# A state-space layer whose scale and shift are read from PSUM, with the skip weight in the kernel's first tap and the residual added on TensorE

## The chip, the cores and the metric

The kernel runs on one core of one Trainium2 chip. The metric is device time in microseconds (us) of one execution, and lower is better. Five engines run side by side: TensorE (PE in the profile; PEld is its weight load), VectorE (DVE), ScalarE (ACT), GpSimd (POOL) and SyncE (SP), which only issues DMAs here. Each engine executes its own instructions strictly in the order in which they were written; engines meet through semaphores.

## The reference

A two-layer decoder over x of 2 batches x 512 tokens x 128 features: a gated recurrence, cross attention, latent attention with an expert mixture, a selective state-space scan, the layer that is edited here, and a second expert mixture. Each is added to its input and normalised. The edited layer, per batch:

```python
c_t = attn_mean @ V                                    # attention over the context
x = layernorm(x_text, g_norm_in, b_norm_in)
scale_in, shift_in = split(c_t @ W_film_in + b_film_in, 2)
x = x * (1.0 + mod_gate * scale_in) + mod_gate * shift_in
y = irfft(rfft(x, 2*L) * rfft(K, 2*L))[:L] + x * D_skip  # K: 512 taps per feature, from 64 complex states
scale_out, shift_out = split(c_t @ W_film_out + b_film_out, 2)
y = y * (1.0 + mod_gate * scale_out) + mod_gate * shift_out
xt = x_text + y
h = layernorm(xt, g_ffn, b_ffn)
xt = xt + gelu(h @ W1 + b1) @ W2 + b2
return layernorm(xt, g_norm_out, b_norm_out)
```

The caller adds the layer's input once more and normalises (ln5).

## The kernel before

Features lie on the 128 partitions and a batch's 512 tokens along the free axis, so most work is on tiles of 128 x 512 float32: one such tile fills one PSUM bank. The two batches are two **lanes**, a and b, with four PSUM banks each (`own(b, 0)` to `own(b, 3)`) and a set of SBUF tiles (`A(b, n)`; `Xin[b]` is the layer's input). What both need (decay tables, the convolution kernel's taps K and their spectrum) is the shared lane w, which borrows lane a's bank in one place.

Every engine has, for each lane, one program written as a generator: one named **step** (mostly one instruction, or one accumulation group) up to each `yield`. `STEPS` lists the names in order. `done(engine, lane, step)` counts the step on that engine's and lane's semaphore; `after(...)` is the wait for it. An engine's final order is a string in `TURNS`: "a7 w1 a6" takes seven steps of lane a, one of w, six of a (L531 to L535). So a step never runs ahead of an earlier one in its engine's order, ready or not. `TABLES` says before which of ScalarE's steps a table of activation functions (log, gelu, exp, sin; the gates' is sin) is loaded, 42 loads in all (L1204).

Lane a runs ahead of lane b by about one layer. The steps that the change and the prediction touch are these.

- Selective scan, per state i of 16: ScalarE's exponential `aa i`, GpSimd's product `by i` (L2195), VectorE's scan `sc i` (L1878) and product `hc i`; sums of products go on TensorE. `dx` on GpSimd and `rl`, `dl` on VectorE prepare the rows that SP writes to DRAM and reads back spread over the partitions ("AR<-scan"). `X4` and ln4 end it; their result is `Xin`. `s4` adds the residual.
- Kernel taps, lane w: ScalarE's sines and exponentials `eP`, `eQ`; GpSimd's `aP`, `aQ`, `U`, `V` and VectorE's `hu`, `hw`, `P` build two tables for each half; TensorE multiplies them (`kp0`, `kp1`) and ScalarE copies (`kp1`). SP stores the taps in four pieces and loads them back rearranged as `Kdl` (L656 to L663, semaphore `kshuf`), between the rows of lane b's scan. TensorE transposes them (`kt`, L1181 to L1184, in lane a's bank 0) and `kf` makes the spectrum.
- Edited layer, per lane: attention `xb.s` (TensorE, bank 2), `xb.m`, `xb.d`, `xb.u`, `xb.i`, `xb.k`, `xb.p` (VectorE), `xb.t` and the copy `xb.a`; normalised input `lni.x`, `lni.g` in A10; the four products `fl0` to `fl3` (scale in, shift in, scale out, shift out; L1039) into banks 0 to 3; ScalarE's copies `s0` to `s3` with the bias into A4, A5, A6, A8; VectorE's `lni.z` = A10 * A4 and `xin` = A10 + A5 into A2; the transposes `xit`; forward transform `xf0`, `xf1` (L1008); spectrum product `ks`, `kd` (lane a only), `bs` to `yo` (VectorE); inverse transform `inv0`, `inv` (L1061), even and odd tokens in the halves of bank 1; then VectorE's `sk` = A2 * D_skip + bank 1, `fo` = A4 * A6, `fp` = A4 + A8, `xt` = A4 + Xin in two halves. Behind it `lnf` and the feed-forward `w1`, `w2`, `lno`, `s5`, `X5` and ln5.
- Around it: the expert units of the first mixture, with ScalarE's gates `sl` (lane a's end at 236 us), and those of the second (`eg`, gates `el`), which follow the edited layer in each lane.

TensorE's steps of the layer stand at L1022 to L1091, ScalarE's at L1440 to L1482, VectorE's at L1897 to L1996. One line of helpers records most VectorE products (L1553), tensor-scalar operations (L1556), scalar_tensor_tensor (L1559) and reductions (L1562); L1208 is every ScalarE activation and L689 every mean square of a norm. For the edited layer the order of the lanes around 344 us is: lane b's scan ends while lane a is in its transforms, and lane b's layer begins.

Of the kernel before, what the change touches and what calls it, by code (L numbers as in the profile page):

```python
# [22 lines left out]
ALU = mybir.AluOpType  # L23
# [3 lines left out]
B, T, D = 2, 512, 128  # L27
# [37 lines left out]
              "lnf": (3, 0), "lno": (3, 1), "ln5": (3, 2), "ln6": (1, 0), "lnf.c": (2, 1), "ln5.c": (0, 1)}  # L65


def _halves(*names):

    return [n + h for n in names for h, _ in COLS]  # L70
# [93 lines left out]
def _centre(t):  # L164
# [13 lines left out]
        *_halves("ln4.v"), "xb.s", "xb.t", "fl0", "fl1", "fl2", "fl3", "xit",  # L178
# [11 lines left out]
        *_ln("ln4"), "lni.sq", "lni.l", "lni.r", "xb.e", "lni.g", "xb.a", "s0", "s1", "s2", "s3", "xit", "ko", "xo", *_ln("lnf"), *_halves("lnf.g"),  # L190
# [13 lines left out]
        "sk", "fo", "fp", *_halves("xt"), *_halves("lnf.x"), *_halves("lno.x"), *_halves("s5"), *_halves("X5"),  # L204
# [13 lines left out]
            "ed.s", "ed.m"],  # L218
# [15 lines left out]
    "dve":  # L234
# [8 lines left out]
    "act":  # L243
# [6 lines left out]
    "pool":  # L250
        "w12 b3 w1 b2 w1 b1 w37 a1 w1 a4 w1 a7 w1 a4 b1 a1 w1 b16 w1",
# [57 lines left out]
def build(nc, dram, out):  # L309
    lay = layouts()  # L310
    with ExitStack() as ctx:
# [371 lines left out]
        def _(pe):  # L683
# [338 lines left out]
            def state_space(b):  # L1022
# [6 lines left out]
                yield  # L1029
                pe.wait_ge(*after("dve", b, "xb.p"))  # L1030
# [7 lines left out]
                for o in range(4):  # L1038
                    mm(own(b, o), VF[:, b, 128 * o:128 * o + 128], A(b, 3), start=True, stop=True)\  # L1039
                        .then_inc(*done("pe", b, f"fl{o}"))  # L1040
                    yield
                pe.wait_ge(*after("dve", b, "xin"))
                pe.wait_ge(*after("act", b, "s3"))
# [3 lines left out]
                yield  # L1047
                pe.wait_ge(*after("act", b, "xit"))
# [9 lines left out]
                for p in range(2):  # L1058
                    pe.wait_ge(*after("dve", b, ("ye", "yo")[p]))
                    for k in range(NFB):  # L1060
                        last = mm(own(b, 1)[:, HT * p:HT * p + HT], Yf[b][:, NF * p + 128 * k:NF * p + 128 * k + 128],  # L1061
                                  Gh[:, T * k + p:T * k + T:2], start=(k == 0), stop=(k == NFB - 1))
                    last.then_inc(*done("pe", b, ("inv0", "inv")[p]))
                    yield
# [49 lines left out]
            def shared_program():  # L1114
# [66 lines left out]
                pe.wait_ge(kshuf, 16)  # L1181
# [10 lines left out]
        def _(act):  # L1192
# [247 lines left out]
            def state_space(b):  # L1440
# [18 lines left out]
                for o, to in enumerate((4, 5, 6, 8)):  # L1459
                    act.wait_ge(*after("pe", b, f"fl{o}"))  # L1460
                    f(A(b, to), own(b, o), ACT.Identity, (b, f"s{o}"), bias=bfilm[:, o:o + 1])
                    yield
# [88 lines left out]
        def _(dve):  # L1551
# [345 lines left out]
            def state_space(b):  # L1897
# [23 lines left out]
                dve.wait_ge(*after("act", b, "s1"))  # L1921
                tt(A(b, 10), A(b, 10), A(b, 4), ALU.mult, (b, "lni.z"))
                yield
                mine(b, "lni.z")
                tt(A(b, 2), A(b, 10), A(b, 5), ALU.add, (b, "xin"))
# [8 lines left out]
                if not b:  # L1934
# [32 lines left out]
                dve.wait_ge(*after("pe", b, "inv"))  # L1967
                pairs = "p (t two) -> p t two"
                stt(A(b, 4).rearrange(pairs, two=2), A(b, 2).rearrange(pairs, two=2), vec("Ds"),
                    own(b, 1).rearrange("p (two t) -> p t two", two=2), ALU.mult, ALU.add, (b, "sk"))  # L1970
                yield
                mine(b, "sk")
                dve.wait_ge(*after("act", b, "s3"))
                tt(A(b, 4), A(b, 4), A(b, 6), ALU.mult, (b, "fo"))
                yield
                mine(b, "fo")
                tt(A(b, 4), A(b, 4), A(b, 8), ALU.add, (b, "fp"))
                yield
                mine(b, "fp")
                for h, c in COLS:  # L1980
                    tt(A(b, 0)[:, c], A(b, 4)[:, c], Xin[b][:, c], ALU.add, (b, f"xt{h}"))
                    yield
# [59 lines left out]
            def shared_program():  # L2042
# [126 lines left out]
                for h in HALVES:  # L2169
# [15 lines left out]
                    yield  # L2185
                dve.wait_ge(loads["ffn1"], 16)
# [345 lines left out]
```

## Time and profile before

| What | us |
|---|---|
| median of three timed runs | 485.99 (484.13 to 487.59) |
| the profiled execution, its own time | 481.76 |
| its span in the trace | 480.0 |
| TensorE busy | 411.1 (86%) |
| VectorE busy | 331.9 (69%) |
| ScalarE busy | 289.2 (60%) |
| GpSimd busy | 124.9 (26%) |

The span is the time from the first to the last instruction that the profiler records; the execution's own time has 1.8 us more around it. The mean granted clock of TensorE was 0.93 of full speed. Times within the trace are counted from the span's start.

How to read it: a busy share over the whole span says little, because the bound changes from stage to stage. A group row gives the source line, engine, operation, output and inputs by name with partitions x elements, the count, busy time and mean of one; then the idle time of the engine just ahead of such instructions and what ended most of it. A timeline row gives start, duration and, in brackets, the idle time before and its releaser.

### The profile page before, as it was taken

Reading aid. Unit: us, or ns where it says so; the run is one execution under the profiler, and the core shown is the slowest. Engines: PE = TensorE matmul, PEld = TensorE weight load, DVE = VectorE, ACT = ScalarE, POOL = GpSimd, SP = SyncE. Lnnn points to the kernel's source line nnn. Section 1 sums busy time; section 2 is a strip of 40 time slices with the busy share of each in tenths; the row PEclk is TensorE's granted clock in tenths of the full one; section 3 lists DMA queues with packets and bytes.
Section 4 is the critical chain, followed back from the end, with each engine's and each line's share of the span. In section 5 each row is a group of like instructions: output and inputs, shape, how many; then the busy total and the mean of one; then the engine's idle time right before and its main releaser. Section 6 shows DMA issues by size and latency. Waiting matters only on the chain.

```text
span 480.0 us, 5922 instructions
## 1 busy us (share of the span) xinstructions
PE 411.1 (86%) x2035; PEld 201.5 (42%) x2035; DVE 331.9 (69%) x616; ACT 289.2 (60%) x508; POOL 124.9 (26%) x128
## 2 busy tenths in 40 slices
PE   6978988878799999999977884557889899999995
PEld 3444433443345554434443221233666544544442
DVE  1485567799969963562799999899977543574454
ACT  5945697525255678989567897456347576552125
POOL 1200000000482029006965767745100200000000
PEclk9988999988879999999997998657989999999999
DMA  7950000564281000005008967988600001502401
GB/s 262 362 157 32 1 2 0 164 98 152 70 182 17 2 3 4 2 12 165 0 1 231 233 164 222 217 223 253 252 0 1 1 0 22 156 1 54 124 0 44
DMA packets 26109, 46.62 MB, mean 97 GB/s; under 512 B 7397, under 2 KB 12742, under 8 KB 24918
## 3 DMA queue, kind: packets, MB, share of 16 engines
q1 hardware_dynamic: 25972, 46.15, 33.7%
q8 instruction: 16, 0.26, 0.2%
q10 hardware_dynamic: 108, 0.10, 0.1%
q14 instruction: 13, 0.11, 0.1%
HBM read 41.13 MB, written 5.01 MB: 96 GB/s over the span
## 4 chain that ended last, share of the span: by engine, by line
PE 59%; DVE 21%; ACT 10%; issue 6%; POOL 2%; DMA 1%; DVEq 0%; SPq 0%; ACTq 0%
PE PS L925 7%; DVE AR L1553 7%; PE PS L957 6%; ACT AR L1208 6%; PE PS L930 5%; PE PS L853 4%; PE PS L839 4%; ACT L1204 3%; PE PS L689 3%; PE PS L822 3%; DVE stats L1562 3%; DVE AR L1878 3%; PE PS L1008 2%; PE PS L1061 2%; DVE AR L1559 2%
## 5 line engine op out<-in xcount | busy, mean ns | idle before, releaser
L1208 ACT ACTIVATE AR<-PS 128x512 f32<-128x512 f32 (+1 forms) x219 | 110.6, 537 | 109.1 <-PE PS L925 49.3
L1553 DVE TENSOR_TENSOR AR<-PS,AR 128x512 f32<-128x512 f32 (+1 forms) x104 | 69.1, 675 | 49.6 <-PE PS L930 30.6
L2195 POOL TENSOR_TENSOR AR<-AR 128x512 f32<-128x512 f32 (+2 forms) x48 | 52.3, 1097 | 136.0 <-DVE AR L1553 106.4
L1208 ACT ACTIVATE AR<-AR 128x256 f32<-128x256 f32 (+2 forms) x130 | 54.5, 469 | 44.6 <-DVE AR L1553 28.1
L1204 ACT ACT_TABLE_LOAD x42 | 53.9, 1283 | 0.8
L1562 DVE TENSOR_REDUCE stats<-PS 128x1 f32<-128x512 f32 (+4 forms) x88 | 43.6, 521 | 8.7 <-PE PS L763 3.5
L1878 DVE TENSOR_TENSOR_SCAN AR<-PS,AR 128x512 f32<-128x512 f32 x32 | 38.8, 1211 | 0.7 <-POOL AR L2195 0.6
L822 PE MATMUL PS<-RR 97*128 97x512 bf16 (+3 forms) x128 | 33.3, 337 | 5.5 <-DVE stats L1562 3.6
L689 PE MATMUL PS<-AR,W_sq 128*128 128x256 f32 x88 | 27.3, 424 | 10.6 <-ACT AR L1208 6.3
L1553 DVE TENSOR_TENSOR AR<-AR 128x512 f32<-128x512 f32 (+2 forms) x48 | 30.7, 654 | 3.6 <-ACT AR L1208 2.3
L839 PE MATMUL PS<-RR 100*128 100x512 bf16 (+3 forms) x128 | 29.8, 303 | 2.2 <-ACT AR L1208 2.1
L2279 POOL TENSOR_TENSOR RR<-KL,lags 128x512 f32<-128x512 f32 x24 | 29.4, 1263 | 1.2 <-PE PS L842 1.1
L930 PE MATMUL PS<-x_in,RR 128*128 128x512 f32 x56 | 28.6, 596 | 0.0
L957 PE MATMUL PS<-AR,RR 128*128 128x512 f32 x56 | 28.5, 596 | 0.0
L925 PE MATMUL PS<-x_in,RR 128*128 128x512 f32 x56 | 28.4, 595 | 0.0
L1208 ACT ACTIVATE PS<-AR,RA 128x512 f32<-128x512 f32 x32 | 21.5, 685 | 10.3 <-DMA AR<-scan 5.1
L689 PEld LDWEIGHTS PS<-AR,W_sq 128*128 128x128 f32 x88 | 15.9, 201 | 24.8 <-ACT AR L1208 16.2
L825 PE MATMUL PS<-W_bf 128*128 128x256 bf16 (+1 forms) x80 | 22.4, 280 | 0.0
L853 PE MATMUL PS<-AR,Vaug 128*9 128x512 f32 (+3 forms) x256 | 21.8, 434 | 0.0
L842 PE MATMUL PS<-W_bf 128*128 128x256 bf16 (+1 forms) x80 | 20.2, 253 | 0.0
L1710 DVE TENSOR_REDUCE stats<-PS 128x1 f32<-128x384 f32 x32 | 17.5, 548 | 3.5 <-PE PS L825 3.3
L822 PEld LDWEIGHTS PS<-RR 97*128 97x128 bf16 x128 | 11.5, 105 | 20.0 <-DVE stats L1562 11.0
(239 smaller groups left out, 697.5 us busy)
## 6 DMA issues: line engine op xcount, KB each, us to landing
AR<-scan SPq DMA_DIRECT2D x64, 256.0 KB, 4.0
RR<-in_ffn SPq DMA_DIRECT2D x1, 2688.0 KB, 11.5
RR<-in_ones SPq DMA_DIRECT2D x2, 832.0 KB
RR<-in_ones SPq DMA_DIRECT2D x2, 784.0 KB
RA<-in_moe SPq DMA_DIRECT2D x1, 1539.5 KB, 6.4
AR<-weights SPq DMA_DIRECT2D x6, 256.0 KB, 4.7
W_mla<-in_mla SPq DMA_DIRECT2D x1, 1504.0 KB, 15.3
W_late<-in_late SPq DMA_DIRECT2D x1, 1076.0 KB, 11.8
```

The lines of the kernel that those rows point to most:

```text
L689: mm(own(b, i)[:, c], w("sq", "ones"), A(b, 1)[:, c], start=True, stop=True)\
L822: mm(ring[:, c:c + n_], Qst[b][0:MROWS, h, 128 * qt:128 * qt + 128], Kst[b][0:MROWS, h, 0:n_], start=(qt, c) == segs[0][1:], stop=False)
L839: mm(ring[:, c:c + n_], Kst[b][0:KROWS, h, 128 * kb:128 * kb + 128], Qst[b][0:KROWS, h, 128 * kb:T], start=(c == 0), stop=False)
L925: mm(own(b, 0), w(group, "g", 128 * k, 128), x, start=True, stop=True)\
L930: mm(own(b, 1), w(group, "u", 128 * k, 128), x, start=True, stop=True)\
L957: mm(own(b, 3), w(group, "d", 128 * j, 128), A(b, 6 + j % 2), start=(j == 0 and base is None), stop=(k == n))\
L1204: nc.scalar.preload_act_table_set(tables[loaded[0]])
L1208: nc.scalar.activation(out_, in_, func, bias=bias, scale=scale).then_inc(*done("act", *step))
L1553: nc.vector.tensor_tensor(out_, a, b_, op).then_inc(*done("dve", *step))
L1562: nc.vector.tensor_reduce(out_, a, X, op).then_inc(*done("dve", *step))
L1878: nc.vector.tensor_tensor_scan(A(b, 14 + i % 2), own(b, 1 + 2 * (i % 2)), scan_row(b, "dx", i), 0.0, ALU.mult, ALU.add).then_inc(*done("dv ...
L2195: nc.gpsimd.tensor_tensor(out_, a, b_, op).then_inc(*done("pool", *step))
```

## The change

- **Scale and shift in.** `s0` and `s1` go. VectorE's `lni.z` and `xin` become scalar_tensor_tensor, which read the products fl0 and fl1 where TensorE left them (banks 0 and 1) and add the bias themselves.
- **Scale and shift out.** The order of the products becomes fl0, fl1, fl3, fl2; fl3 goes to bank 2 and fl2 to bank 3, and ScalarE copies fl3 first, then fl2.
- **The input.** A new TensorE step `fx` multiplies `Xin` by the identity into bank 2 and leaves the sum open; fl3 is added to it. So A8 holds shift out plus x_text, and `xt` adds A8 in place of `Xin`; `fp` goes.
- **The skip weight.** A new VectorE step `kD` (lane w) adds half of D_skip to the first column of `Kdl`, once the rows are loaded back; the transform's later steps hold a factor of two. TensorE's `kt` waits for `kD`. `sk` goes.
- **Two halves.** The odd tokens of the inverse transform go to bank 3. `fo0` and `fo` multiply the even and the odd tokens, 128 x 256 each, from PSUM by A6 into every second column of A4.
- **New turns.** All four strings of `TURNS` are new from the first step on, and `TABLES` with them: 48 loads for 42. Moves beside the edited steps, as the two strings give them: VectorE takes b's hc3 ahead of a's X4, b's sc5 and hc5 ahead of a's xb.m, the shared P1 ahead of a's sc11 and so of b's rl and dl, hu3, hw3, hu4 and hw4 ahead of a's sc4, a's yi ahead of b's X4, a's ye and yo ahead of b's xb.m, and a's fo0 and fo ahead of b's xb.p. GpSimd takes dx, by0 and by1 of lane a ahead of aP1, by2 to by4 ahead of aQ1, and U11, U21, V1 later between the by's; the chain of decay products (dc1 to dc23) ahead of lane b's split of keys and queries. ScalarE takes kp1 ahead of b's aa2, and part of lane b's norm f1 (its log and root) in between a's gates sl4 to sl7, with a table load ahead of each of the two and one behind it. TensorE takes a's lnf.c ahead of b's fl0.

```diff
+FILM_BANKS, FILM_TURNS = (0, 1, 3, 2), (0, 1, 3, 2)
...
-        *_halves("ln4.v"), "xb.s", "xb.t", "fl0", "fl1", "fl2", "fl3", "xit",
+        *_halves("ln4.v"), "xb.s", "fx", "xb.t", "fl0", "fl1", "fl3", "fl2", "xit",
...
-        "sk", "fo", "fp", *_halves("xt"), ...
+        "fo0", "fo", *_halves("xt"), ...
...                                              (TensorE, state_space)
+                pe.wait_ge(*after("dve", b, "xb.d"))
+                mm(own(b, 2), w("sq", "id"), Xin[b][:, :], start=True, stop=False).then_inc(*done("pe", b, "fx"))
+                yield
...
-                for o in range(4):
-                    mm(own(b, o), VF[:, b, 128 * o:128 * o + 128], A(b, 3), start=True, stop=True)\
+                for o in FILM_TURNS:
+                    mm(own(b, FILM_BANKS[o]), VF[:, b, 128 * o:128 * o + 128], A(b, 3), start=(o != 3), stop=True)\
                         .then_inc(*done("pe", b, f"fl{o}"))
                     yield
+                pe.wait_ge(*after("act", b, "s3"))
                 pe.wait_ge(*after("dve", b, "xin"))
-                pe.wait_ge(*after("act", b, "s3"))
...
+                pe.wait_ge(*after("act", b, "s2"))
                 pe.wait_ge(*after("act", b, "xit"))
...
-                        last = mm(own(b, 1)[:, HT * p:HT * p + HT], Yf[b][...],
+                        last = mm(own(b, (1, 3)[p])[:, HT * p:HT * p + HT], Yf[b][...],
...                                              (TensorE, shared lane)
-                pe.wait_ge(kshuf, 16)
+                pe.wait_ge(*after("dve", "w", "kD"))
                 pe.wait_ge(*after("act", "w", "kp1"))
...                                              (ScalarE)
-                for o, to in enumerate((4, 5, 6, 8)):
+                for o, to in ((3, 8), (2, 6)):
                     act.wait_ge(*after("pe", b, f"fl{o}"))
-                    f(A(b, to), own(b, o), ACT.Identity, (b, f"s{o}"), bias=bfilm[:, o:o + 1])
+                    f(A(b, to), own(b, FILM_BANKS[o]), ACT.Identity, (b, f"s{o}"), bias=bfilm[:, o:o + 1])
...                                              (VectorE, state_space)
-                dve.wait_ge(*after("act", b, "s1"))
-                tt(A(b, 10), A(b, 10), A(b, 4), ALU.mult, (b, "lni.z"))
+                dve.wait_ge(*after("pool", "w", "bf1"))
+                dve.wait_ge(*after("act", b, "lni.g"))
+                dve.wait_ge(*after("pe", b, "fl0"))
+                stt(A(b, 10), own(b, FILM_BANKS[0]), bfilm[:, 0:1], A(b, 10), ALU.add, ALU.mult, (b, "lni.z"))
                 yield
                 mine(b, "lni.z")
-                tt(A(b, 2), A(b, 10), A(b, 5), ALU.add, (b, "xin"))
+                dve.wait_ge(*after("pe", b, "fl1"))
+                stt(A(b, 2), own(b, FILM_BANKS[1]), bfilm[:, 1:2], A(b, 10), ALU.add, ALU.add, (b, "xin"))
...
-                dve.wait_ge(*after("pe", b, "inv"))
-                pairs = "p (t two) -> p t two"
-                stt(A(b, 4).rearrange(pairs, two=2), A(b, 2).rearrange(pairs, two=2), vec("Ds"),
-                    own(b, 1).rearrange("p (two t) -> p t two", two=2), ALU.mult, ALU.add, (b, "sk"))
-                yield
-                mine(b, "sk")
-                dve.wait_ge(*after("act", b, "s3"))
-                tt(A(b, 4), A(b, 4), A(b, 6), ALU.mult, (b, "fo"))
-                yield
+                dve.wait_ge(*after("act", b, "s2"))
+                for p in range(2):
+                    dve.wait_ge(*after("pe", b, ("inv0", "inv")[p]))
+                    tt(A(b, 4)[:, p:T:2], own(b, (1, 3)[p])[:, HT * p:HT * p + HT], A(b, 6)[:, p:T:2], ALU.mult, (b, ("fo0", "fo")[p]))
+                    yield
                 mine(b, "fo")
-                tt(A(b, 4), A(b, 4), A(b, 8), ALU.add, (b, "fp"))
-                yield
-                mine(b, "fp")
                 for h, c in COLS:
-                    tt(A(b, 0)[:, c], A(b, 4)[:, c], Xin[b][:, c], ALU.add, (b, f"xt{h}"))
+                    tt(A(b, 0)[:, c], A(b, 4)[:, c], A(b, 8)[:, c], ALU.add, (b, f"xt{h}"))
...                                              (VectorE, shared lane, after P1)
+                dve.wait_ge(kshuf, 16)
+                stt(Kdl[:, 0:1], vec("Ds"), 0.5, Kdl[:, 0:1], ALU.mult, ALU.add, ("w", "kD"))
+                yield
```

In this diff the words in brackets behind the dots name the engine whose program follows.

## Rows read from the trace of the kernel before

**Rows 1.** Windows cut where the bound changes; us, busy us of PE, PEld, DVE, ACT, POOL, PEclk, DMA, GB/s
```profile
0.00:132.00 132.00, 108.36 (x416) 52.70 (x417) 89.87 (x185) 76.36 (x148) 10.02 (x22) 0.93 0.39 118
132.00:240.00 108.00, 102.92 (x728) 50.01 (x727) 68.16 (x151) 78.17 (x136) 48.98 (x57) 0.97 0.18 43
240.00:344.00 104.00, 73.85 (x513) 34.02 (x511) 97.52 (x131) 67.53 (x102) 62.70 (x50) 0.82 0.73 206
344.00:386.00 42.00, 36.94 (x153) 24.82 (x154) 28.94 (x49) 24.44 (x50) 3.18 (x1) 0.96 0.01 4
386.00:478.00 92.00, 89.06 (x230) 40.00 (x228) 47.45 (x104) 42.66 (x73) 0.00 (x0) 1.00 0.18 49
```

**Rows 2.** Groups by line and form: VectorE, 344 to 386 us (busy us, mean ns)
```profile
L1553 DVE TENSOR_TENSOR AR<-AR 128x512 f32<-128x512 f32 x10 | 6.8, 688 | 1.3 <-ACT AR L1208 1.2
...
L1553 DVE TENSOR_TENSOR AR<-AR,x_in 128x256 f32<-128x256 f32 x4 | 1.6, 422 | 0.1
L1559 DVE SCALAR_TENSOR_TENSOR AR<-AR,W_vec,PS 128x512 f32<-128x512 f32 x2 | 1.5, 746 | 1.0 <-PE PS L1061 1.0
L1553 DVE TENSOR_TENSOR AR<-PS,AR 128x256 f32<-128x256 f32 x3 | 1.2, 421 | 3.1 <-ACT AR L1208 3.1
```

**Rows 3.** Timeline of TensorE, 343 to 387 us (start us, us, [idle us before <-releaser])
```profile
348.74 0.49 PE L1026 MATMUL PS<-M,x_in 128*128 128x128 f32 x2 [1.65 <-DVE x_in L1553]
...
350.15 5.42 PE L1061 MATMUL PS<-RR,AR 128*128 128x256 f32 x16
...
356.69 1.98 PE L1039 MATMUL PS<-AR,VF 128*128 128x512 f32 x4 [0.69 <-ACT AR L1208]
...
361.69 0.71 PE L1045 MATMUL PS<-W_sq,AR 128*128 128x128 f32 x4 [0.44 <-ACT AR L1208]
...
366.77 3.60 PE L1075 MATMUL PS<-AR,W_late 128*128 128x512 f32 x8
...
380.82 1.13 PE L689 MATMUL PS<-AR,W_sq 128*128 128x256 f32 x4 [0.82 <-ACT AR L1208]
382.55 1.13 PE L1067 MATMUL PS<-AR,W_sq 128*128 128x256 f32 x4 [0.60 <-DVE AR L1553]
```

**Rows 4.** Waits of VectorE, 240 to 344 us (us in total, times, longest us)
```profile
DVE x_in L1553 <- ACT AR L1208: 1.5, 1, 1.5
...
DVE AR L1553 <- ACT AR L1208: 0.7, 2, 0.5
...
DVE AR L1556 <- ACT AR L1208: 0.5, 1, 0.5
DVE stats L1562 <- PE PS L1027: 0.5, 1, 0.5
```

**Rows 5.** Timeline of GpSimd, 228 to 306 us
```profile
231.30 15.86 POOL L2279 TENSOR_TENSOR RR<-KL,lags 128x512 f32<-128x512 f32 x12
...
265.15 2.08 POOL L2279 TENSOR_TENSOR RR<-RR,KL 128x512 f32<-128x512 f32 x2
267.18 2.51 POOL L2195 TENSOR_TENSOR AR<-AR 128x512 f32<-128x512 f32 x2
```

**Rows 6.** Timeline of VectorE, 272 us: lane b's sc5
```profile
272.25 1.21 DVE L1878 TENSOR_TENSOR_SCAN AR<-PS,AR 128x512 f32<-128x512 f32 x1
```

**Rows 7.** Timeline of TensorE, 304 to 345 us: the transpose of the kernel rows
```profile
317.93 1.12 PE L1184 MATMUL PS<-W_sq,stats 128*128 128x128 f32 x4 [0.31 <-DMA stats<-kernel_rows]
```

**Rows 8.** Timeline of VectorE, 354 us: lane b's xb.p
```profile
354.14 0.69 DVE L1553 TENSOR_TENSOR AR<-AR,stats 128x512 f32<-128x512 f32 x1
```

**Rows 9.** Timeline of ScalarE: a copy of half a bank, one of a whole
```profile
240.60 0.38 ACT L1208 ACTIVATE AR<-PS 128x256 f32<-128x256 f32 x1 [0.73 <-PE PS L957]
...
356.04 0.60 ACT L1208 ACTIVATE AR<-PS 128x512 f32<-128x512 f32 x1 [2.78 <-PE PS L1032]
```

**Rows 10.** The page's costliest groups (busy us, mean ns, idle us before)
```profile
L1204 ACT ACT_TABLE_LOAD x42 | 53.9, 1283 | 0.8
```

**Rows 11.** The page's chain that ended last, shares of the span by line
```profile
PE PS L925 7%; DVE AR L1553 7%; PE PS L957 6%; ACT AR L1208 6%; PE PS L930 5%; PE PS L853 4%; PE PS L839 4%; ACT L1204 3%; PE PS L689 3%; PE PS L822 3%; DVE stats L1562 3%; DVE AR L1878 3%; PE PS L1008 2%; PE PS L1061 2%; DVE AR L1559 2%
```

More of the change, by code:

```diff
@@ L189 @@
         "ab", "ex", "sp", "bB", "bC", *[f"aa{i}" for i in _N],
-        *_ln("ln4"), "lni.sq", "lni.l", "lni.r", "xb.e", "lni.g", "xb.a", "s0", "s1", "s2", "s3", "xit", "ko", "xo", *_ln("lnf"), *_halves("lnf.g"),
+        *_ln("ln4"), "lni.sq", "lni.l", "lni.r", "xb.e", "lni.g", "xb.a", "s3", "s2", "xit", "ko", "xo", *_ln("lnf"), *_halves("lnf.g"),
         "u0", "u1", "u2", "u3", *_ln("lno"), *_ln("ln5"), "rt1",
@@ L203 @@
         "xb.m", "xb.d", "lni.x", "xb.u", "xb.i", "xb.k", "xb.p", "lni.z", "xin", "ks", "kd", "bs", "bd", "xr", "xi", "yr", "yi", "ye", "yo",
-        "sk", "fo", "fp", *_halves("xt"), *_halves("lnf.x"), *_halves("lno.x"), *_halves("s5"), *_halves("X5"),
+        "fo0", "fo", *_halves("xt"), *_halves("lnf.x"), *_halves("lno.x"), *_halves("s5"), *_halves("X5"),
         "mx", "ms", "su", "iv", "pr1", *_PICK1[:5], *_E1[0], *_PICK1[5:9], *_E1[1], *_PICK1[9:],
@@ L217 @@
             *[f"{n}{h}" for h in HALVES for n in ("r1.", "q1.", "r2.", "q2.", "rQ0.", "qQ0.", "rQ1.", "qQ1.", "P")],
-            "ed.s", "ed.m"],
+            "kD", "ed.s", "ed.m"],
     "pool": ["kz", "va0", "va1", "fb.r", "fb.s", "fb.c", "bh", "bf", "bf1", "wz0", "wz1", "la", *[f"dc{i}" for i in range(1, 24)], "wb", "wc", "sz", "hd.c",
@@ L226 @@
     "pe":
[7 rows of a table removed]
-    "dve":
[8 rows of a table removed]
-    "act":
[6 rows of a table removed]
[7 rows of a table added]
+    "dve":
[8 rows of a table added]
+    "act":
[6 rows of a table added]
     "pool":
-        "w12 b3 w1 b2 w1 b1 w37 a1 w1 a4 w1 a7 w1 a4 b1 a1 w1 b16 w1",
+        "w38 b6 w11 a3 w1 a3 w1 a2 w1 a1 w1 a1 w1 a6 b1 a1 w1 b16 w1",
 }
 TABLES = (
[4 rows of a table removed]
[4 rows of a table added]
 def steps_of(engine, lane):
@@ L1060, in state_space @@
                     for k in range(NFB):
-                        last = mm(own(b, 1)[:, HT * p:HT * p + HT], Yf[b][:, NF * p + 128 * k:NF * p + 128 * k + 128],
+                        last = mm(own(b, (1, 3)[p])[:, HT * p:HT * p + HT], Yf[b][:, NF * p + 128 * k:NF * p + 128 * k + 128],
                                   Gh[:, T * k + p:T * k + T:2], start=(k == 0), stop=(k == NFB - 1))
```

50 rows, old and new, of tables (TABLES, TURNS) are left out of this document.

## The prediction

> **What bounds the kernel now.** I read the windows view first, cut where the bound changes [rows 1]. Of 132 us at the start no engine is full (TensorE 108.4, VectorE 89.9 busy). From 132 to 240 TensorE is busy 102.9 of 108, from 240 to 344 VectorE 97.5 of 104, from 344 to 386 TensorE 36.9 of 42 and from 386 to 478 TensorE 89.1 of 92. The edited layer lies across the last three: lane a's part of it runs inside lane b's selective scan (before 344, VectorE the bound), lane b's in the short stretch to 386, where TensorE has waits left; behind it stands dense TensorE work that the change does not shorten. So two things can move the end: VectorE's own time and waits before 344, and TensorE's waits between 344 and 386.
>
> The execution that I sum against took 481.76 us, with a span of 480.0; the median of the three timed runs is 485.99, so it stands 4.2 us below that median. The differences are taken over unchanged.
>
> **Part 1: what the layer's arithmetic saves.** Per lane VectorE loses sk (0.75), one of two products (fo, 0.69) and fp (0.69) [rows 2] (its AR<-AR and SCALAR_TENSOR_TENSOR rows) and gets two products over 256 columns from PSUM instead (0.42 each, same rows): 2.13 becomes 0.84 or, if a step of two elements costs, at most 1.5 (two whole 0.75). I take 0.84, as the replaced sk also read with a step of two and cost only 0.06 more than its neighbours. lni.z and xin become scalar_tensor_tensor, 0.75 for 0.69: +0.12 for lane a. ScalarE loses two copies per lane; it is busy 24.4 of 42 us in the layer's stretch [rows 1], so that is worth something only where a copy stood before a reader. TensorE gets one product of 128x512 per lane (fx): 3.60 us for four such (the trace counts them as eight) [rows 3], so 0.9. Lane a's falls into a TensorE wait for VectorE before 344 and costs nothing there; if VectorE no longer covered it, 0.9. The one new instruction kD has 128x1 outputs: between 0 and the 0.42 of a 128x256; I take 0.2.
>
> On reading from PSUM: the rows show 421 ns with a PSUM operand and 422 without, both over 256 columns [rows 2], so I charge nothing. The Trainium skill, "VectorE: DVE Perf Modes", section on the TRN2 errata, speaks against the change: it counts 120 cycles of fixed cost for a PSUM source against 58 for SBUF, at 0.96 GHz. By it the four reads per lane would cost an estimated 0.5 us in all, and the sum below would end near -0.2 instead of -0.7.
>
> **Part 2: the stretch to 344.** VectorE's waits there are few [rows 4]: 1.5 us where lane a's X4 waits for ScalarE; 0.5 at xb.m; 0.5 and, of the 0.7, another 0.5 at lane b's rl and dl. The new turns put b's hc3 (0.7, AR<-AR of [rows 2]) ahead of X4 and b's sc5 and hc5 ahead of xb.m: -0.7 and -0.5. They put the kernel table's P1 ahead of rl, so that VectorE works while ScalarE is awaited: -1.0. Against that, GpSimd's aP1 and aQ1 move from before the scan's feed into it: half of the 12 instructions that took 15.86 us [rows 5], so 7.9 us. by5 ended at 269.7, behind the two of U21 (2.08, same rows); behind aP1 and aQ1, with U21 now after it, it ends at 269.7 + 7.9 - 2.1 = 275.5 at the latest. VectorE read it in sc5 at 272.25 [rows 6]; hu4 and hw4, pulled forward at 0.69 each, make that 273.6. The stall is between 0 (the feed catches up in its own DMA waits) and 1.9; I take 1.5, nearer the upper end because nothing but those DMA waits gives way. Behind sc5 the feed has recovered by P1, as V1 was waited for by nobody.
>
> kD stands in VectorE's queue behind a's xb.d and waits for the kernel rows' DMA; before, only TensorE's transpose waited for it, 0.31 us, until 317.93 [rows 7]. Behind kD wait lni.x, hc6 and the rest of the scan. ScalarE's kp1 goes ahead of aa2 and aa3, so SP's four row stores and the load back are issued about 1 us sooner, and VectorE reaches kD later than 318. I cost the wait at nothing; each us that the load is late is a us of the whole. Sum of part 2: 0.2 + 0.12 - 2.2 + 1.5 = -0.4.
>
> **Part 3: from 344 to 386, lane b.** TensorE works from 348.74 on, but for 0.69 before fl0, 0.44 before xit, 0.82 before ln5.v and 0.60 before lnf.c [rows 3]. In the new order VectorE does a's yi (0.7) before b's X4, so xb.s and the inverse transform, 5.42 us of TensorE to 355.6, move back to 356.3. fo waits for the end of that transform, and b's xb.p is queued behind fo. xb.p ended at 354.83 [rows 8]; now 356.3 + 0.42 + 0.69 = 357.4. Then the transpose (0.71 for such a one), ScalarE's copy (0.60, [rows 9]) and fl0 at 358.7 instead of 356.69: +2.0. In that time TensorE does fx (0.9) and a's two halves of lnf.c, which stood inside the fl block before (as many columns as fx, so 0.9); the block ends 2.0 - 0.9 = 1.1 later. The 0.44 before xit goes, because the eviction that it waited for now follows the third product, not the fourth: +0.7. The dense run to 380 keeps +0.7. There, sk (0.75) no longer stands before s5 and fo (0.42) does: the wait of 0.82 takes up 0.3. The wait of 0.60 for xta goes entirely, as b's chain after the inverse is short by two whole instructions, and part of the first half's wait follows: +0.7 - 0.3 - 0.6 - 0.1 = -0.3. Where a wait goes, ln5.r on ScalarE and then X5 are the next late thing. If fx's cover were gone, fx would be 0.9 more.
>
> **Part 4: the other turns.** All four queues have new orders from the first step on. In the two stretches where TensorE is full an order that keeps the same steps can move little, and before 132 the moves that I followed cancel (a's norm is sooner, the shared table steps stand in front of its next users). I take 0; the ends are given by the rivals.
>
> **Sum:** -0.4 - 0.3 + 0 = -0.7 us: 481.1 for an execution like the profiled one, 485.3 for the median. Call it no change: this kernel's timings can tell about 1% (4.9 us).
>
> **Rivals.**
> (a) TensorE is full and only pays. fx is 0.9 more, fo holds up xb.p as above, and the waits of 0.82 and 0.60 stay because ScalarE's norm sets them: +0.7 + 0.9 in part 3, so 485.99 - 0.4 + 1.6 = 487.2. For it: from 348.74 on TensorE has only 2.55 us of waits. Against: the 0.60 is put down to VectorE's xta, which does get sooner. Chance 0.18.
> (b) The table loads: slower. The new list has 48 loads for 42. Four of the six lie in lane a's expert units between 228 and 240, where the norm of lane b is now cut in between the gates. One unit then needs of ScalarE two loads, a gate and a piece of the norm, 2 x 1.28 + 0.60 + 0.38 = 3.5 us [rows 9, 10], against three TensorE products of 0.9. From the point at which ScalarE arrives last at each unit, the four loads are on the path: 4 x 1.283 = 5.1, which is 491.1. For: loads make up 3% of the chain that ended last, 14.4 us of their 53.9 [rows 10, 11], so a load is on the path about once in four; six would give +2.1 by that share. Against: lane b's norm is needed only after the units end, and eP0 and eQ0 already stood there. Chance 0.14, with the loss above 1%. The Trainium skill, "ScalarE: Activation LUTs", section on table sets, has the rule for it: batch activation calls by set; the new order breaks it at these units.
> (c) The new turns win at the start. Before 132 TensorE is idle 23.6 us and nothing is full [rows 1]; shared steps move there into VectorE's idle time, and lane b's split runs without the decay chain's pieces between. A fifth of the idle time would be 4.7: 481.76 - 0.7 - 4.7 = 476.4, or 480.6 on the median. Against: an earlier lane b meets a full TensorE from 132 on. Chance 0.24.
> (d) The edit does not do what it says: kD or fo waits longer than what it replaced. It is in (a) and in part 2's wait.
>
> **Numbers.** Forecast 0.44, (a) 0.18, (b) 0.14, (c) 0.24. Faster by over 1%: (c), 0.24, for a fifth or more of that idle time. Slower by over 1%: (b), 0.14. Within: forecast and (a), 0.62. The range takes in (a), half-way results of (b) and most of (c): 479.5 to 491.0. Around the forecast alone, with part 2's stall from 0 to 1.9, a wait at kD of up to 2 and the median's own spread of 1.9, it is 482 to 488.
>
> **What would show it.** Right: after the inverse transform two products of 128x256 from PSUM and no 128x512 between it and xta; fl0 about 2 us behind the inverse, with fx and lnf.c between; the wait of 0.60 before lnf.c gone; VectorE's share from 240 to 344 a little higher and its wait at X4 halved. Wrong: a VectorE wait for a DMA before lni.x; a wait for GpSimd at sc5 above 2 us; TensorE waits for ScalarE between 228 and 240 that were not there; or lane b's first maxima more than 2 us away from their old time.

## The result

The changed kernel takes 489.92 us (median of 14 runs, 486.26 to 495.84), the kernel before 484.29 us (14 runs, 481.59 to 489.31): a ratio of 1.0106, 95% interval [1.0071, 1.0141]. The medians are of all timed executions; the ratios here and below leave out the few that ran in a slower state. The changed kernel is slower by 1%, some 5 us, where I had forecast no change. The profiled execution took 489.39 us with a span of 487.6.

The windows of the changed kernel, cut where TensorE has done the same products as at the cuts of [rows 1] (columns as there), with one cut more, at 158.0 us, which is 155.6 us in the kernel before:

```profile
0.00:132.20 132.20, 108.88 (x416) 51.87 (x417) 90.55 (x186) 77.99 (x149) 23.39 (x47) 0.94 0.39 119
132.20:158.00 25.80, 23.82 (x166) 11.72 (x166) 21.35 (x50) 10.72 (x20) 3.09 (x3) 0.86 0.43 88
158.00:248.40 90.40, 82.52 (x563) 38.21 (x562) 46.67 (x101) 70.70 (x117) 30.67 (x28) 0.98 0.08 25
248.40:351.40 103.00, 73.77 (x515) 33.61 (x513) 95.43 (x133) 67.26 (x103) 60.14 (x50) 0.87 0.74 207
351.40:392.70 41.30, 37.77 (x156) 25.07 (x157) 25.98 (x46) 23.17 (x48) 0.00 (x0) 0.96 0.01 5
392.70:485.60 92.90, 89.12 (x230) 39.90 (x228) 49.07 (x105) 45.33 (x75) 3.18 (x1) 1.00 0.17 49
```

Against [rows 1] the stretches differ by +0.2, +8.2 (the second and third line together), -1.0, -0.7 and +0.9 us, 7.6 in all, which is the difference of the spans. The two stretches in which the edited layer lies became shorter. The loss is in TensorE's full stretch from 132 us on, where the change edits no instruction and only the order is new.

Of the +8.2, 2.2 arise up to 158.0 us, and they can't be put down to the change. Lane b's maxima product mx7.D, a little further on, is a step by which TensorE has done the same products in all sixteen traces. Three of them have the old order up to there and end it at 172.8 to 175.7 us; thirteen have the new one and end it at 173.1 to 179.9 (the kernel before 172.8, the changed one 175.3). So executions of one order differ by more than 2.2 us there. The other 6.0 arise behind 158 us. From mx7.D to fg1, a product of lane a's first mixture, and from fg1 to lane b's router product, the windows of the kernel before (first two lines) and of the changed one, with the same products in each pair, are (us, busy PE, PEld, DVE, ACT, POOL, PEclk, DMA, GB/s):

```profile
172.81:208.97 36.16, 34.91 (x293) 16.33 (x295) 16.59 (x40) 29.70 (x60) 15.48 (x13) 1.00 0.01 2
208.97:243.12 34.15, 31.03 (x136) 14.05 (x139) 19.28 (x32) 27.14 (x42) 23.40 (x20) 1.00 0.20 62
```
```profile
175.27:215.88 40.61, 35.84 (x293) 16.66 (x295) 18.27 (x45) 31.13 (x62) 12.59 (x12) 0.98 0.01 2
215.88:251.70 35.82, 32.18 (x126) 13.83 (x127) 18.04 (x28) 31.25 (x44) 18.08 (x16) 0.97 0.19 59
```

The first part is 4.5 us longer, with TensorE idle 4.8 us in place of 1.3; the second is 1.7 us longer.

Inside this stretch, ten-microsecond windows of the kernel before and of the changed one (same columns):

```profile
195.00:205.00 10.00, 9.30 (x78) 4.68 (x77) 4.21 (x10) 8.62 (x21) 0.00 (x0) 1.00 0.01 2
205.00:215.00 10.00, 8.94 (x59) 3.55 (x58) 6.01 (x19) 8.50 (x14) 0.00 (x0) 1.00 0.00 1
215.00:225.00 10.00, 10.00 (x35) 4.52 (x35) 3.91 (x7) 9.72 (x10) 6.51 (x6) 1.00 0.67 212
```
```profile
195.00:205.00 10.00, 8.33 (x72) 4.21 (x72) 5.01 (x10) 7.20 (x17) 0.00 (x0) 1.00 0.00 0
205.00:215.00 10.00, 8.33 (x66) 3.40 (x58) 6.41 (x17) 7.99 (x13) 0.00 (x0) 0.97 0.01 3
215.00:225.00 10.00, 9.67 (x55) 3.32 (x57) 2.55 (x9) 6.76 (x11) 0.00 (x0) 0.86 0.02 7
```

TensorE and ScalarE are both less busy, and the granted clock leaves 1.00: 3.4 us across the last two windows, from 214.4, ran at 1.2 instead of 2.4 GHz. Three waits of TensorE there, from its timeline (start us, us, [idle before <-releaser]):

```profile
201.83 0.39 PE L840 MATMUL PS<-RR 100*128 100x512 bf16 x1 [1.02 <-ACT AR L1213]
211.18 0.39 PE L840 MATMUL PS<-RR 100*128 100x384 bf16 x2 [0.27 <-ACT AR L1213]
214.07 1.80 PE L926 MATMUL PS<-AR,RA 128*128 128x512 f32 x2 [1.40 <-ACT AR L1213]
```

and, from the chain that ended last, the part through the first of these (start us, us, what):

```profile
199.81 1.00 PE PS L968 x8
200.84 0.20 DVE stats L1558
201.09 0.07 issue
201.19 0.59 ACT AR L1213
201.83 0.39 PE PS L840
```

Read downwards: lane a's router product (L968), VectorE's router step, ScalarE, and then lane b's softmax copy, on which lane b's next product waits. Lane b needs nothing of lane a's router; it stands behind it on ScalarE, as that engine's timeline shows:

```profile
201.06 0.23 ACT L1213 ACTIVATE stats<-stats 128x28 f32<-128x28 f32 x1 [2.41 <-DVE stats L1558]
201.19 4.10 ACT L1213 ACTIVATE AR<-PS 128x512 f32<-128x512 f32 x7
...
212.12 1.28 ACT L1209 ACT_TABLE_LOAD   x1
213.42 0.60 ACT L1213 ACTIVATE AR<-PS 128x512 f32<-128x512 f32 x1
```

The new turns take the router's exponential rt twelve softmax blocks earlier, ahead of su20 in place of behind su31. They also take TensorE's first expert products fg0 and fu0 earlier, so nothing is left to run while the table is loaded for the gate sl0, and fg1 waits 1.40 us (0.29 before) and then takes 1.80 us at the lower clock (1.12 before).

### The profile page after: what moved, and what is told of

Read it like the earlier page. It is cut to its first block, busy times and chain, and to the rows that moved or that the text cites. A ratio compares the mean times of both kernels' runs of the same rounds, so it can differ in the third digit from the quotient of the medians.

```text
span 487.6 us, 5935 instructions
## 1 busy us (share of the span) xinstructions
PE 415.9 (85%) x2039; PEld 200.4 (41%) x2039; DVE 329.1 (67%) x615; ACT 295.2 (61%) x510; POOL 120.5 (25%) x128
## 4 chain that ended last, share of the span: by engine, by line
PE 60%; DVE 17%; ACT 11%; DMA 5%; issue 4%; POOL 2%; SPq 1%; ACTq 0%; DVEq 0%
ACT AR L1213 7%; PE PS L926 7%; PE PS L931 6%; PE PS L958 6%; DVE AR L1558 5%; PE PS L840 4%; PE PS L854 4%; PE PS L690 3%; DVE AR L1883 3%; PE PS L727 3%; ACT L1209 3%; PE PS L823 3%; POOL AR L2199 2%; PE PS L1009 2%; DMA AR<-scan 2%
## 5 line engine op out<-in xcount | busy, mean ns | idle before, releaser
L1213 ACT ACTIVATE AR<-PS 128x512 f32<-128x512 f32 (+2 forms) x219 | 110.4, 535 | 103.7 <-PE PS L926 39.8
L1558 DVE TENSOR_TENSOR AR<-PS,AR 128x512 f32<-128x512 f32 (+1 forms) x108 | 71.2, 669 | 62.2 <-PE PS L931 31.1
L2199 POOL TENSOR_TENSOR AR<-AR 128x512 f32<-128x512 f32 (+2 forms) x48 | 53.2, 1119 | 42.3 <-DMA AR<-scan 27.5
L1567 DVE TENSOR_REDUCE stats<-PS 128x1 f32<-128x128 f32 (+4 forms) x88 | 43.7, 525 | 10.9 <-PE PS L826 5.6
L2283 POOL TENSOR_TENSOR RR<-KL,lags 128x512 f32<-128x512 f32 x24 | 25.3, 1085 | 33.1 <-PE PS L843 33.0
L1558 DVE TENSOR_TENSOR AR<-AR 128x512 f32<-128x512 f32 (+3 forms) x44 | 27.7, 648 | 2.1 <-ACT AR L1213 0.7
L926 PE MATMUL PS<-AR,RA 128*128 128x512 f32 x32 | 18.4, 660 | 2.0 <-ACT AR L1213 1.9
```

What stands on the lines that cost most here:

```text
L926: mm(own(b, 0), w(group, "g", 128 * k, 128), x, start=True, stop=True)\
L1213: nc.scalar.activation(out_, in_, func, bias=bias, scale=scale).then_inc(*done("act", *step))
L1558: nc.vector.tensor_tensor(out_, a, b_, op).then_inc(*done("dve", *step))
L1567: nc.vector.tensor_reduce(out_, a, X, op).then_inc(*done("dve", *step))
L2199: nc.gpsimd.tensor_tensor(out_, a, b_, op).then_inc(*done("pool", *step))
```

## The experiments

All ratios are to the kernel before, timed on the same chip, with 6 to 12 executions of each variant. "Old order" and "new order" are the orders of the two kernels' turns.

**1. The edit alone.** The changed code in the old turns.

```diff
-TURNS = {...}   # the new strings, 48 table loads
+TURNS = {...}   # before's, with fx ahead of xb.t, kD behind a's xb.d, fo0 in sk's place; 42 loads
```

> The whole arithmetic edit (fx, the PSUM reads, kD, the split products, 42 table loads) in the turns of before; kD directly behind lane a's xb.d, fx directly ahead of xb.t. Theory 1 (the new turns ahead of 240 us lose the time, the edit is worth about -1): 483 to 484.5 where before takes 484.3, so a ratio of 0.997 to 1.000. Theory 2 (the edit itself costs: fx 1.8 us on TensorE for both lanes, kD's wait for the kernel rows): 487 to 490. Theory 3 (the four table loads between lane a's gates lose it): as theory 1 here.

Measured 483.67 us, 0.9999 [0.9975, 1.0024]. The arithmetic edit costs nothing and, in the old turns, brings nothing. Theory 2 falls.

**2. The turns alone.** The old code in the new turns.

```diff
+ the new strings, without fx and kD; s0, s1 directly ahead of s2; sk, fo, fp together in the place of fo
```

> The arithmetic of before (s0 to s3, sk, fo, fp, no fx, no kD) in the new turns, 48 table loads. Theory 1: 490 to 491, ratio 1.010 to 1.015, the time after 300 us a little worse than with the edit. Theory 2: 484 to 486. Theory 3: as theory 1 here.

Measured 499.42 us, 1.034 [1.0309, 1.0371]: worse than every theory had it, and not a clean test of the layer. VectorE's timeline at lni.z of lane a and of lane b:

```profile
339.74 1.43 DVE L1535 TENSOR_TENSOR AR<-AR 128x512 f32<-128x512 f32 x1 [2.23 <-ACT AR L1190]
374.05 1.42 DVE L1535 TENSOR_TENSOR AR<-AR 128x512 f32<-128x512 f32 x2 [2.82 <-ACT AR L1190]
```

The re-inserted copies s0 and s1 come only when ScalarE reaches the place of s3, and VectorE's queue stands behind lni.z until then, in both lanes. The new turns are made for a layer without these copies. For the stretch ahead of the layer the run is a clean test: from mx7.D to lane b's router product its trace takes 76.4 us, as the changed kernel's does, against 70.3 before. There the turns alone make the loss.

**3. Old order up to 240 us, new order behind it,** with the changed code.

```diff
-# every engine: the new order from the start
+# every engine: the steps done by 249 us in the old order, the rest in the new one (44 loads)
```

> The edited arithmetic; every engine takes all steps that the changed kernel has done by 249 us in the order of before, and from there on the new turns; 44 table loads. Theory 1: 482 to 484, below before, since the stretch from 240 to 300 gained some 2 us in the changed kernel's trace and the layer 1.4. Theory 2: 487 or more. Theory 3: as theory 1.

Measured 480.86 us, 0.9945 [0.9919, 0.997]: faster than both kernels. The late part of the new turns, with the edit, is worth some 3 us; the early part loses more than that. From mx7.D to lane b's router product the traces of this run and of run 1 take 70.2 and 70.3 us, as before the change.

**4. The table loads at the gates.**

```diff
-# ScalarE: ... sl4  f1.la  sl5  f1.l  sl6  sl7 ...
+# ScalarE: ... sl4  sl5  sl6  sl7  f1.la  f1.l ...   (lane a's gates, lane b's norm; 44 loads)
```

> The changed kernel, with the two logs of lane b's norm f1 behind lane a's gate sl7 instead of between sl4 and sl7: 44 table loads for 48, nothing else moved. Theory 3 (the loads at the gates are on the path): 485 to 486, 4 to 5 us below the changed kernel, ratio to before 1.000 to 1.003. Theory 1 (the loss is made ahead of sl4): at most 1 us below the changed kernel, 489 to 490. Theory 2: 489 to 490.

Measured 490.28 us, 1.0114 [1.0074, 1.0155]. Removing the four loads between the gates gives nothing back in the time; from fg1 to lane b's router product the trace takes 35.4 us for the changed kernel's 35.8, where theory 3 had 4 to 5. Theory 3, my rival (b), falls: its time was nearly right and its reason wrong. The Trainium skill, "ScalarE: Activation LUTs", section on table sets, says to batch calls by set; here four loads fewer, 5.1 us of ScalarE, were not to be seen in the time.

**5. Only the steps from 185 to 249 us in the old order.**

```diff
-# all engines: the new order
+# all engines: the new order to 185 us, the old one to 249, the new one behind it (44 loads)
```

> The changed kernel with only the steps that it does between 185 and 249 us put in the order of before (44 table loads); all before and behind stays new. Theory 1a (the whole loss is made in this one stretch, where lane a's first expert units run beside lane b's attention): 481 to 482.5, as old turns up to 240 gave 480.9. Rival 1b (the new order ahead of 185 us loses as well, by the lower clock from 100 to 150): 484 to 486.

Measured 483.32 us, 0.996 [0.9925, 0.9996]: the whole loss comes back from this stretch, to between what theory 1a and rival 1b forecast. Whether the new order ahead of 185 us costs anything is open: run 3, which has the old order there too, came out at 0.9945, and the two intervals overlap. The windows of run 5, beside those above, are at full clock again:

```profile
195.00:205.00 10.00, 9.30 (x75) 4.28 (x73) 4.13 (x6) 9.11 (x22) 1.18 (x2) 1.00 0.01 2
205.00:215.00 10.00, 9.71 (x70) 4.43 (x69) 7.09 (x22) 7.63 (x15) 0.00 (x0) 1.00 0.00 1
215.00:225.00 10.00, 9.23 (x54) 3.82 (x53) 3.71 (x8) 9.75 (x14) 1.83 (x2) 1.00 0.32 94
```

**6. One ScalarE step moved back.**

```diff
-# ScalarE: ... b.su19  a.rt  b.su20 ... b.su31 ...
+# ScalarE: ... b.su19  b.su20 ... b.su31  a.rt ...
```

> The changed kernel with one ScalarE step moved: lane a's router exponential rt, which stands ahead of lane b's su20 and holds ScalarE for 2.4 us until VectorE has the router's maxima, goes behind su31, where it stood before. Theory 2a (this wait on ScalarE starves TensorE of softmax blocks; 1.0 us of TensorE idle at su22 and the smaller ones ahead of su30): 1.5 to 2 us less than the changed kernel, 487.5 to 488.5. Rival 2b (the table load ahead of gate sl0 is uncovered and decides, so that time saved here is waited for there): no change, 489.5 to 490.

Measured 490.73 us, 1.0103 [1.0051, 1.0155]: no gain. ScalarE's wait went, and TensorE's timeline has another in its place:

```profile
212.94 1.08 PE L852 MATMUL PS<-W_sq,AR 128*128 128x128 f32 x4 [4.61 <-DVE AR L1540]
```

VectorE's order was planned for the early rt: its step pd waits for rt, 6.4 us here, and lane b's ri1 and y1, which TensorE needs for yT2, are queued behind pd.

**7. The first expert products moved back.**

```diff
-# TensorE: ... b.su22  a.fg0 ... b.su27  a.fu0 ... b.su33  b.su34 ...
+# TensorE: ... b.su22 ... b.su27 ... b.su33  a.fg0  b.su34  a.fu0 ...
```

> The changed kernel with two TensorE steps moved: lane a's first expert products fg0 and fu0 go from behind su22 and su27 to behind su33 and su34, where they stood before, so that 1.8 us of products stand again between su33 and fg1, which waits 1.4 us for gate sl0 behind its table load. Rival 2b: that wait and the half clock behind it go, 2 to 3 us less than the changed kernel, 487 to 488. Theory 2a: 0 to 1 us less, since lane b's softmax stays late.

Measured 488.7 us, 1.0063 [1.003, 1.0096]. The wait at fg1 is gone from its timeline, and about 0.4% with it, which is not clear of noise: the intervals of the two kernels overlap.

**8. Both moves.**

```diff
+# ScalarE and TensorE: a.rt behind b.su31; TensorE: fg0, fu0 as in 7
```

> The changed kernel with both moves, and TensorE's rt behind su31 too. If the two mechanisms add: 4 to 5 us less than the changed kernel, 485 to 486. If they share one wait: as the better of the two alone.

Measured 491.79 us, 1.013 [1.0076, 1.0184]. The two do not add: the wait for VectorE at yT2 is there again (4.5 us).

**9, 10. The stretch cut at 203 us.**

```diff
+# 9: only the steps from 185 to 203 us in the old order (48 loads)
+# 10: only the steps from 203 to 249 us in the old order (44 loads)
```

> The changed kernel with the order of before only for the steps that it does between 185 and 203 us (24 to 28 places move on TensorE and ScalarE, 7 on VectorE): lane a's router exponential, its first expert products and lane b's softmax blocks su4 to su22. Theory 3a (the loss adds up along the stretch; in the changed kernel's trace 1.7 of the 5.6 us arise here): 1.5 to 2 us less than the changed kernel, 488 to 488.5. Rival 3b (the waits here only start the half-clock spell and the rest behind them): all of the 6.6 us that the whole stretch gives back, 483 to 484. Rival 3c (the later part sets the time alone): no change, 490.

> The changed kernel with the order of before only for the steps that it does between 203 and 249 us (44 places on TensorE, 32 on VectorE, 20 on ScalarE; 44 table loads). Theory 3a: 4 to 5 us less than the changed kernel, 485 to 486. Rival 3b: 0 to 2 us less, 488 to 490. Rival 3c: 483 to 484.

Measured 490.85 us, 1.0156 [1.0099, 1.0213], and 487.02 us, 1.0086 [1.005, 1.0121]. None of the three theories fits both. At 203 us the two orders don't meet: the first variant leaves a 3.0 us wait at TensorE's rt, at the seam.

**11, 12. The router's chain on ScalarE and VectorE together,** and with fg0 and fu0 late as well.

```diff
+# 11: ScalarE a.rt behind b.su31; VectorE b.ri1, b.y1 ahead of a.pd
+# 12: the same, and TensorE's fg0, fu0 as in 7
```

> The changed kernel with three steps moved, all of one chain: ScalarE's rt of lane a behind lane b's su31, and on VectorE lane b's ri1 and y1 ahead of lane a's pd, which waits for rt. With rt alone moved, TensorE had waited 4.6 us at yT2 for VectorE, whose ri1 and y1 were queued behind pd. Theory 4 (lane b's attention is held up by lane a's router wherever the two meet on an in-order engine, so the hold-up must go from ScalarE and VectorE together): 2 to 3 us less than the changed kernel, 487 to 488, with the 1.4 us at fg1 still there. Rival (the first part of the stretch costs nothing, only the units behind it do): 489.5 to 490.5.

> As the run before, and TensorE's fg0 and fu0 behind su33 and su34. Theory 4 with the wait at fg1 covered too: 4 to 6 us less than the changed kernel, 484 to 486. Rival: 488 to 489, as with fg0 and fu0 alone (488.7).

Measured 489.94 us, 1.012 [1.0087, 1.0153], and 489.24 us, 1.0104 [1.0059, 1.0148]: theory 4 as I had put it, that these few steps are the whole hold-up, falls. The 4.6 us at yT2 are gone, and in run 12 the 1.4 at fg1 too, but VectorE now comes later to the first unit's product and fu1 waits for it:

```profile
221.67 1.12 PE L913 MATMUL PS<-AR,RA 128*128 128x512 f32 x2 [2.43 <-DVE AR L1540]
```

**13, 14. The stretch cut at 216 us,** where both orders have done the same steps on TensorE up to fg1.

```diff
+# 13: only the steps from 185 to 216 us in the old order (48 loads)
+# 14: only the steps from 216 to 249 us in the old order (44 loads)
```

> The changed kernel with the order of before for the steps that it does between 185 and 216 us, that is lane b's softmax and lane a's router up to the product fg1; 48 table loads, the split norm between the gates stays. Theory 5 (the loss is made where lane a's router meets lane b's attention, before the gates; 4.5 of the 5.6 us of TensorE's lag in the changed kernel's trace arise from 185 to 212): 4 to 5 us less than the changed kernel, 485 to 486. Rival 5b (the gates behind it, with their loads and the norm in between, hold whatever is gained earlier): 488 to 490.

> The changed kernel with the order of before only from 216 to 249 us: lane a's units from fu1 on, the gates and the norm behind them, 44 table loads. Theory 5: at most 1 us less, 489 to 490. Rival 5b: 485 to 487.

Measured 486.02 us, 1.0039 [1.001, 1.0068], and 488.03 us, 1.0078 [1.0042, 1.0115]. By the medians the first part gives back 3.9 us of the 6.6 and the second 1.9, the second not clear of noise. The traces say the same of the stretch itself (us from mx7.D to fg1, from there to lane b's router product, both, and how long the granted clock was at 1.2 GHz within them):

| Kernel | to fg1 | behind it | both | at 1.2 GHz |
|---|---|---|---|---|
| before | 36.2 | 34.2 | 70.3 | 0 |
| changed | 40.6 | 35.8 | 76.4 | 3.4 |
| run 4 (norm behind the gates) | 42.1 | 35.4 | 77.4 | 6.8 |
| run 5 (old from 185 to 249) | 36.8 | 34.0 | 70.8 | 0 |
| run 10 (old from 203 to 249) | 39.8 | 34.0 | 73.8 | 0 |
| run 12 (router's chain, fg0, fu0) | 38.4 | 38.0 | 76.3 | 0 |
| run 13 (old from 185 to 216) | 36.8 | 36.0 | 72.9 | 0 |
| run 14 (old from 216 to 249) | 42.3 | 34.1 | 76.4 | 6.8 |

The old order gives back 3.8 us where it stands ahead of fg1 and some 1.7 behind it, each without the other. The larger share of the loss is made where lane a's router meets lane b's softmax, ahead of the gates; theory 5 holds for the first part and puts the second too low.

The table also tells what the lower clock does. Runs 4 and 14 keep the changed kernel's order on every engine ahead of fg1 and show the same waits there; a spell of 3.4 us at 1.2 GHz fell into this part of each (from 204.9 and 202.5 us), and it took 1.5 and 1.6 us longer. So such a spell cost some 1.5 us by itself. The loss does not need one: runs 10 and 12 ran at full clock in both parts and still took 3.5 and 6.0 us more than the kernel before.

What stays open: which waits of the stretch carry the loss. Taking away one showed another (runs 6 to 8, 11 and 12), so the two waits followed above are shown as waits, not as the price of the order. One engine alone in the old order was not tried.

## Why the prediction was wrong

The step that failed is **part 4**: "In the two stretches where TensorE is full an order that keeps the same steps can move little", and "I take 0". TensorE was busy 102.9 of 108 us there [rows 1]. I read this as cover; it is the opposite. A full engine leaves at most 5.1 us to gain and sets no such bound on the loss: a hand-over between lanes that comes later can open a wait in it. Measured: +6.0 us behind 158 us in the profiled execution, 6.6 by the medians of run 5. I did list that the orders were new, but the moves that stand in this stretch (lane a's rt, fg0 and fu0 ahead of lane b's softmax blocks) are missing from the moves under "The change", and I did not follow them. The other half of part 4 held: TensorE reached the products of 132.0 us at 132.2.

**Rival (b)** gave 491.1 and the right sign, on the wrong mechanism (run 4). That the measured 489.92 lies inside the range of 479.5 to 491.0 is luck: the range reached so far up for (a) and for half of (b), and neither mechanism occurred. **Rival (c)**, a gain at the start, did not come: lane b was earlier (its first maxima at 140.3 us for 143.5, one of the signs named for being wrong), lane a later, and TensorE had done the same work at 132.2. **Rival (a)** did not come either: fx stands in TensorE's waits in both lanes.

**Part 1** held in its terms, from the groups of VectorE in the layer's stretch:

```profile
L1558 DVE TENSOR_TENSOR AR<-PS,AR 128x256 f32<-128x256 f32 x8 | 3.2, 423 | 9.8 <-PE PS L1066 5.2 <-ACT AR L1213 4.5
L1558 DVE TENSOR_TENSOR AR<-AR 128x256 f32<-128x256 f32 x4 | 1.5, 417 | 0.0
L1564 DVE SCALAR_TENSOR_TENSOR AR<-PS,small,AR 128x512 f32<-128x512 f32 x2 | 1.5, 751 | 0.1
```

The two products with a step of two cost 0.42 each, so the step costs nothing; lni.z and xin 0.75. The fixed extra cost of a PSUM source, which by the cycles that the Trainium skill gives ("VectorE: DVE Perf Modes", section on the TRN2 errata) would be an estimated 65 ns, was 6 ns in this pair of rows; the measurement decides. The step kD was mis-sized: 0.67 us, above my upper bound of 0.42 (see the last section).

**Part 2**: the stretch came out at -1.0 for -0.4. VectorE's wait at X4 fell from 1.5 to 0.2, and kD was no wait on VectorE: it follows xb.d at once. VectorE's share did not rise, as I had named for being right, but fell from 97.5 of 104 us to 95.4 of 103. The row at 272.25 us, headed lane b's sc5 in [rows 6], is lane a's (lane b's ends at 317.6), so the feed that part 2 speaks of is lane a's. The stall of the scan's feed came, but not at sc5. VectorE's waits for GpSimd's products in the stretch of the changed kernel:

```profile
DVE AR L1883 <- POOL AR L2199: 3.9, 4, 1.4
```

They stand at the first two scans of each lane, 3.9 us in all against 0.6 before; I had 1.5.

**Part 3**: -0.7 for -0.3. From TensorE's timeline, lane b:

```profile
362.81 1.02 PE L1032 MATMUL PS<-x_in,W_sq 128*128 128x512 f32 x2
364.09 0.66 PE L1036 MATMUL PS<-W_sq,AR 128*128 128x128 f32 x4 [0.26 <-DVE AR L1558]
364.58 1.03 PE L1072 MATMUL PS<-AR,W_sq 128*128 128x256 f32 x4
365.45 3.69 PE L1043 MATMUL PS<-AR,VF 128*128 128x512 f32 x8
369.11 0.74 PE L1049 MATMUL PS<-W_sq,AR 128*128 128x128 f32 x4
...
388.07 1.13 PE L690 MATMUL PS<-AR,W_sq 128*128 128x256 f32 x4 [0.59 <-ACT AR L1213]
389.04 1.03 PE L1072 MATMUL PS<-AR,W_sq 128*128 128x256 f32 x4
```

These are fx, xb.t, lane a's lnf.c, the four products from fl0 on, xit, ln5.v and lane b's lnf.c. From the start of xb.s (356.15) to fl0 it is 9.3 us against 7.95 in [rows 3]: +1.35, the forecast's 2.0 less the 0.7 by which xb.s itself was to move. In that time fx and lnf.c ran, as said. The waits before fl0, xit and lnf.c are gone, and 0.82 became 0.59.

## What to carry to other kernels

Where an engine is busy 95% of a stretch, a new order of the same work can gain at most the idle 5% of that stretch, and nothing bounds its loss in the same way (here 6%), so follow each lane's chain through the in-order engine that it shares with the other lane and ask what stands behind a step that waits. Test an edit and a new order apart, then cut the new order in time: here the edit in the old turns was even, and old turns in the full stretch with new ones behind it beat both kernels (0.9945). Cut only where both orders have done the same steps, and move whole stretches, since a single step put back found the other engines planned without it (runs 6 and 8). Compare traces between points at which both kernels have done the same products: here that told 1.7 us apart where the medians could not.

## What was not expected of the hardware

The product kD writes one element per partition and took 0.67 us, as long as a product over 512. It ran beside one of GpSimd's products, and it ended when that one did (327.3 us; VectorE's row, then GpSimd's):

```profile
326.67 0.67 DVE L1564 SCALAR_TENSOR_TENSOR stats<-W_vec,stats 128x1 f32<-128x1 f32 x1
326.06 1.27 POOL L2199 TENSOR_TENSOR AR<-AR 128x512 f32<-128x512 f32 x1 [1.63 <-DMA AR<-scan]
```

In run 14 no product of GpSimd was running, and the same instruction took 0.15 us:

```profile
325.33 0.15 DVE L1546 SCALAR_TENSOR_TENSOR stats<-W_vec,stats 128x1 f32<-128x1 f32 x1
323.99 1.26 POOL L2181 TENSOR_TENSOR AR<-AR 128x512 f32<-128x512 f32 x1 [1.72 <-DMA AR<-scan]
```

Over the fourteen traces with kD it took 0.15 us in four and 0.28 to 1.10 in ten, and in each of the ten it ended within 0.02 us of the GpSimd product that was running when it started. So this step cost what was left of a GpSimd instruction.

The granted clock fell between 205 and 225 us in the changed kernel, after waits of 1.02, 0.27 and 1.40 us, and not in the kernel before, whose waits in the same work were 0.70, 0.29 and 0.57 us, nor in runs 5 and 13. It did not fall in runs 10 and 12 either, although TensorE waited 1.02 and 0.75 us in the one and 2.43 in the other, so what brings it down is not shown.
